# One core's attention and expert layers: the engines' orders run one group further ahead, with ScalarE's logarithm in front of the casts of a later group

## The chip, the cores and the metric

The kernel runs on one core of a Trainium2 chip. A core has TensorE (PE), VectorE (DVE), ScalarE (ACT), GpSimd (POOL) and SyncE (SP, which here only issues DMAs). Each engine works through its own list of instructions in order, and the lists meet in semaphores. The metric is the device time of one execution in microseconds (us), the median of several runs.

## The reference

Input is 8 sequences of 512 rows of 256 numbers. The first half is a causal attention layer with a layer norm, which the change doesn't touch. The second half, over the same 4096 rows, is an expert layer:

```python
logits = gelu(xf @ router_w1 + router_b1) @ router_w2 + router_b2   # two of 8 experts per row
for _ in range(2):                                                  # ITERS
    ctx = concat(integrated, v)
    shared_ctrl = gelu(ctx @ shared_w1 + b) @ shared_w2 + b
    x_sh, v_sh = inl(shared_ctrl, integrated, v, mu)
    ctrl = experts(ctx per chosen expert)                           # same shape, an expert's own weights
    x_r, v_r = inl(ctrl, ...), weighted sum over the two experts
    halt = sigmoid(gelu(integrated @ halt_w1 + b) @ halt_w2 + b)
    integrated, v += halt * (mix of shared and routed - old)
refined = gelu(integrated @ refine_w1 + b) @ refine_w2 + b
out = layernorm(x + xf + integration_weight * refined)

def inl(ctrl, xs, vs, mu):                                          # a, b, g: thirds of ctrl
    v_next = sigmoid(a) * vs - softplus(b) * (xs - mu)
    return xs + 0.1 * sigmoid(g) * v_next, v_next
```

## The kernel before

The function `experts` works in steps of 512 rows: a *group* is 512 rows in their own order (8 groups), a *quad* is 4 tiles of 128 rows sorted by expert, each tile with one expert's weights (18 quads). Its stages, one after the other, are: the router and the first shared pass; the first routed pass (18 quads, work numbers n from W_B); the second shared pass (8 groups, from W_S2); the second routed pass (18 quads, from W_D); and the refinement with the last norm (8 groups). The change touches the last four.

A step n of a pass goes through the engines like this.

- TensorE turns the rows (`turn`, L1941: transposes in fp32, 2 chunks in the first iteration, 4 in the second) into a ring of four PSUM banks (`ring`). The order of all fills of that ring is written out in the list FILLS (L1097).
- ScalarE casts each chunk to fp16 (`casts`, L1393). VectorE subtracts the cast from the chunk, which gives the low parts (`lows`, L1558), and with that frees the bank.
- TensorE makes the hidden layer from high and low parts (`routed_hidden`, L2047, 28 matmuls of 128 columns in the first routed pass and 52 in the second; `token_hidden`, L2093, 18 matmuls of 512 columns). For a quad it first reads the experts' numbers into registers (`quad_experts`, L2043). It begins only when all low parts are there (`ready`).
- ScalarE applies gelu twice (`gelu_hidden`, L1407: once in fp32, once in fp16), and VectorE makes the low half of the fp16 pair (`hidden`, L1567: a copy, L1570, and a subtraction, L1571).
- TensorE makes the control values (`control`, L1970) in two PSUM slots: two tiles to a slot in the first iteration, one in the second. A slot is free again when it has been read.
- ScalarE reads them (`tanhs`, L1431: tanh and, in the second iteration, relu for each of 4 tiles), loads the table of the logarithm, takes one logarithm over the step's 4 x 256 columns, and loads the gelu table again (`logs`, L1460). In front of the logarithm VectorE takes the absolute value in place (`absolute`, L1720).
- GpSimd subtracts and multiplies (`products`, L1294: two tensor_tensor instructions, L1300 and L1302). VectorE finishes the step (`velocity`, L1739, three instructions; `first_velocity` in the first iteration), and the result is stored, or added to the state (`add_shared2`, L1828).

In the second shared pass VectorE also adds up the routed results of the first iteration (`combine1`, L1804: 16 instructions a group, from rows that GpSimd gathers with indirect DMAs, `gather1`), and the halting gate is made: TensorE's `cl` fill (L2105), VectorE's `halts` (L1816), ScalarE's tanh (L1488), VectorE's `weigh` (L1824). The second routed pass gathers its rows with `gather_state` (L1327).

Before the change, the loop of each pass has in step n, on ScalarE: casts of step n+1, tanhs n, logs n, gelu n+1. On TensorE: turn n+1, control n, hidden n+1. On VectorE: lows n+1, absolute n, (combine1 n+2), velocity n-1, hidden n+1. The hidden pair h_hl, h_h1 has one buffer. In the refinement, a group's transposes, hidden layer and output follow each other on TensorE.

Of the kernel before, what the change touches and what calls it, by code (L numbers as in the profile page):

```python
# [868 lines left out]
def experts(nc, w, normed_dram, out):  # L869
# [7 lines left out]
    with ExitStack() as ctx:  # L877
# [63 lines left out]
        h_hl = sb("h_hl", [P, TOK], F16)  # L941
        h_h1 = sb("h_h1", [P, TOK], F16)
# [158 lines left out]
        for q in range(QUADS):  # L1101
            FILLS += [f"bx{q}_{c}" for c in range(KC)] + [f"bh{q}"]
        for g in range(GROUPS):
            FILLS += [f"cx{g}_{c}" for c in range(2 * KC)] + [f"cr{g}", f"cs{g}", f"cl{g}"]
        for q in range(QUADS):
            FILLS += [f"dx{q}_{c}" for c in range(2 * KC)] + [f"dh{q}"]
        for g in range(GROUPS):
            FILLS += [f"ex{g}_{c}" for c in range(KC)] + [f"eh{g}_{c}" for c in range(RC)]
# [118 lines left out]
        def _(pool):  # L1227
# [91 lines left out]
            for t in range(2 * NT):  # L1319
                gather1(t)  # L1320
            for g in range(GROUPS):
                for t in range((g + 2) * NT, min((g + 3) * NT, TILES)):
                    gather1(t)
                products(W_S2 + g, xs[:, g * NT:(g + 1) * NT, 0:D])


            def gather_state(q):  # L1327
                if q == 3:
                    pool.wait_ge(ew_done, W_D)
# [6 lines left out]

            for g in range(GROUPS):
                pool.wait_ge(xv_stored[g], 32)
            pool.wait_ge(comb_done, TILES)
            AHEAD = D_RING - 2  # L1340
            for q in range(AHEAD):
                gather_state(q)
            for q in range(QUADS):
                products(W_D + q, xg_it2(q)[:, :, 0:D])
                if q + AHEAD < QUADS:
                    gather_state(q + AHEAD)

# [29 lines left out]
        def _(act):  # L1377
# [96 lines left out]
            casts("b", 0, KC)  # L1474
            gelu_hidden(W_B, "bh0", h_hl[:], False)
            for q in range(QUADS):
                if q + 1 < QUADS:
                    casts("b", q + 1, KC)
                tanhs(W_B + q)
                logs(W_B + q)  # L1480
                if q + 1 < QUADS:
                    gelu_hidden(W_B + q + 1, f"bh{q + 1}", h_hl[:], False)

            def token_hidden(g):
                gelu_router(f"cr{g}", f"cl{g - 1}" if g else f"rl{GROUPS - 1}")
                gelu_hidden(W_S2 + g, f"cs{g}", h_hl[:], True)
# [3 lines left out]

            casts("c", 0, 2 * KC)
            token_hidden(0)
            for g in range(GROUPS):
                if g + 1 < GROUPS:
                    casts("c", g + 1, 2 * KC)
                tanhs(W_S2 + g)
                logs(W_S2 + g)
                if g + 1 < GROUPS:
                    token_hidden(g + 1)

            casts("d", 0, 2 * KC)
            gelu_hidden(W_D, "dh0", h_hl[:], False)
            for q in range(QUADS):
                if q + 1 < QUADS:
                    casts("d", q + 1, 2 * KC)
                tanhs(W_D + q)
                logs(W_D + q)
                if q + 1 < QUADS:
                    gelu_hidden(W_D + q + 1, f"dh{q + 1}", h_hl[:], False)
# [6 lines left out]
            act.wait_ge(ew_done, EWS)  # L1516
            for g in range(GROUPS):
                casts("e", g, KC)
                if g:
                    act.wait_ge(ctrl_filled[(uses(EWS) + g - 1) % 2], (uses(EWS) + g - 1) // 2 + 1)  # L1520
                    rstd(g - 1)
                for c in range(RC):
                    src, free = filled(f"eh{g}_{c}")
                    s.activation(gr32[:, c, :], src, ACT.Gelu, bias=cols[:, 2 + c:3 + c])
                    s.activation(gp[:, 0, c, :], src, ACT.Gelu, bias=cols[:, 2 + c:3 + c]).then_inc(free, 1)
            rstd(GROUPS - 1)

        @block.vector
        def _(dve):
# [259 lines left out]
            lows("b", 0, KC)  # L1789
            keep_ids(0)  # L1790
            hidden(W_B, "bh0", h_hl, h_h1)
            for q in range(QUADS):
                if q + 1 < QUADS:
                    lows("b", q + 1, KC)
                    keep_ids(q + 1)
# [4 lines left out]
                if q + 1 < QUADS:  # L1800
                    hidden(W_B + q + 1, f"bh{q + 1}", h_hl, h_h1)
# [35 lines left out]

            combine1(0)
            lows("c", 0, 2 * KC)
            combine1(1)  # L1840
            hidden(W_S2, "cs0", h_hl, h_h1)
            halts(0)
            for g in range(GROUPS):
                if g + 1 < GROUPS:
                    lows("c", g + 1, 2 * KC)
                absolute(W_S2 + g)
                weigh(g)
                if g + 2 < GROUPS:
                    combine1(g + 2)
                if g:  # L1850
                    velocity(W_S2 + g - 1, vs[:, (g - 1) * NT:g * NT, :])
                    add_shared2(g - 1)
                if g + 1 < GROUPS:
                    hidden(W_S2 + g + 1, f"cs{g + 1}", h_hl, h_h1)
# [344 lines left out]
```

## Time and profile before

| | us |
|---|---|
| median of 3 runs | 1744.98 (1744.79 to 1745.25) |
| the profiled execution's own time | 1741.15 |
| its span, first to last instruction | 1739.2 |
| first routed pass, first to last logarithm's end (842.10 to 1058.85) | 216.75 |
| second shared pass and the change-over, first logarithm's end to that of the second routed pass (1106.32 to 1306.71) | 200.39 |
| second routed pass, first to last logarithm's end (1306.71 to 1552.55) | 245.84 |
| rest to the end: last products, gathers, refinement | 186.65 |

The times of the stages are cut where ScalarE ends a logarithm, since each step has exactly one; 17 periods lie between the first and the last of 18. The last row of the table ends with the span.

### The profile page before, as it was taken

What the parts mean: (1) busy time and instruction counts of PE and PEld (TensorE: products, weight loads), DVE (VectorE), ACT (ScalarE), POOL (GpSimd) and SP (SyncE); (2) the same over time, 40 slices, a digit from 0 to 9 for tenths busy, and PEclk for the clock granted to TensorE, in tenths of its full rate; (3) what the DMA queues carried; (4) which work ended last, traced back from release to release, by engine and by line L of the source; (5) the groups of instructions that cost most, each with busy time, mean ns of one, the idle gap of its engine ahead of it and who ended that gap; (6) DMA issues with size and microseconds to landing.
All of it is one profiled execution on the core that took longest, in us unless ns stands there. A gap on an engine that the chain in (4) does not pass through costs nothing.

```text
span 1739.2 us, 21709 instructions
## 1 busy us (share of the span) xinstructions
PE 1085.2 (62%) x6930; PEld 648.3 (37%) x6930; DVE 1057.5 (61%) x1951; ACT 845.1 (49%) x1303; POOL 720.3 (41%) x692
## 2 busy tenths in 40 slices
PE   4778887978989456521556551654546666644775
PEld 2334453544544233200423231332225555532443
DVE  1655656666665337566465553888756777764665
ACT  1134534444545334354556652643547777751544
POOL 6012322223223360176233435645266666437451
PEclk9678988998989867665677775876768988876888
DMA  4946357176270395023243424544143333214341
GB/s 88 147 69 104 67 87 118 39 97 106 65 87 14 82 250 180 15 98 115 76 137 110 137 94 146 193 145 134 37 121 97 110 110 110 62 52 139 98 120 59
DMA packets 151755, 178.84 MB, mean 103 GB/s; under 512 B 33207, under 2 KB 127826, under 8 KB 151517
## 3 DMA queue, kind: packets, MB, share of 16 engines
q1 hardware_dynamic: 134624, 124.85, 31.6%
q0 software_dynamic: 17024, 52.58, 10.0%
q8 instruction: 66, 1.08, 0.3%
q14 instruction: 41, 0.34, 0.1%
HBM read 100.25 MB, written 76.87 MB: 102 GB/s over the span
## 4 chain that ended last, share of the span: by engine, by line
DVE 20%; PE 15%; ACT 13%; issue 10%; POOL 5%; DMA 2%; SPq 0%; ACTq 0%; DVEq 0%; POOLq 0%
PE exp_ps L1966 7%; DVE h_hl L1571 4%; ACT ct L1455 3%; DVE xs L1809 2%; DVE vs L1810 2%; PE exp_ps L2055 2%; ACT ct L1445 2%; PE exp_ps L2057 2%; ACT g L1413 1%; PE exp_ps L2056 1%; DVE h_h L1570 1%; ACT L1466 1%; PE exp_ps L2016 1%; DVE ct L1725 1%; ACT h_hl L1414 1%
## 5 line engine op out<-in xcount | busy, mean ns | idle before, releaser
L561 DVE TENSOR_REDUCE neg_max<-att_ps 128x1 f32<-128x512 f32 (+3 forms) x448 | 217.0, 533 | 75.5 <-PE att_ps L730 74.1
L499 ACT ACTIVATE probs<-att_ps 128x512 f32<-128x512 f32 x320 | 175.8, 609 | 172.1 <-PE att_ps L739 171.2
L1300 POOL TENSOR_TENSOR rb<-rb,ct 128x1024 f32<-128x1024 f32 x44 | 108.7, 2471 | 329.4 <-ACT ct L1465 329.4
L729 PE MATMUL att_ps<-k_stack,q_stack 96*128 96x512 bf16 (+3 forms) x512 | 163.3, 360 | 70.5 <-DVE neg_max L561 31.9
L1966 PE MATMUL exp_ps<-w_top,h_hl 128*128 (+2 forms) x280 | 102.1, 428 | 135.6 <-DVE h_hl L1571 117.7
L1399 ACT CAST e_xT<-exp_ps 128x512 f16<-128x512 f32 x172 | 92.5, 607 | 130.3 <-PE exp_ps L1944 130.1
L2055 PE MATMUL exp_ps<-e_xT,w 128*128 128x128 f16 x432 | 112.4, 266 | 57.0 <-issue 56.3
L406 POOL TENSOR_TENSOR wait_carrier<-wait_carrier 128x1 f32<-128x1 f32 x64 | 12.5, 195 | 297.4 <-ACT probs L499 297.4
L739 PE MATMUL att_ps<-q_stack,k_stack 98*128 98x512 bf16 (+3 forms) x512 | 125.4, 319 | 9.4 <-DMA q_stack<-max_parts 7.3
L730 PE MATMUL att_ps<-mask_q,identb 128*128 128x128 bf16 x512 | 126.5, 253 | 0.0
L1564 DVE TENSOR_TENSOR e_xT<-exp_ps,e_xT 128x512 f16<-128x512 f32 x172 | 109.8, 684 | 19.6 <-ACT e_xT L1399 18.2
L1291 POOL DMA_INDIRECT xs_dram<-xs,pos x64 | 68.1, 1064 | 108.7 <-DVE pos L1717 89.5
L2057 PE MATMUL exp_ps<-e_xT,w 128*128 128x128 f16 x432 | 111.8, 265 | 0.0
L2056 PE MATMUL exp_ps<-e_xT,w 128*128 128x128 f16 x432 | 111.1, 263 | 0.0
L729 PEld LDWEIGHTS att_ps<-k_stack,q_stack 96*128 96x128 bf16 x512 | 54.7, 110 | 144.3 <-DVE neg_max L561 93.4
L1445 ACT ACTIVATE ct<-exp_ps 128x1024 f32<-128x1024 f32 x52 | 53.2, 1024 | 110.4 <-PE exp_ps L1966 84.1
L1966 PE MATMUL exp_ps<-w_low,h_h 128*128 (+2 forms) x280 | 100.5, 422 | 0.0
L1966 PEld LDWEIGHTS exp_ps<-w_top,h_hl 128*128 128x128 f16 x280 | 30.0, 112 | 185.1 <-issue 164.0
L1944 PE MATMUL exp_ps<-e_ident,xs 128*128 128x128 f32 x192 | 32.4, 325 | 101.3 <-DVE vs L1810 68.1
L1455 ACT ACTIVATE ct<-exp_ps 128x768 f32<-128x768 f32 x104 | 84.6, 814 | 21.4 <-PE exp_ps L1966 20.4
L1725 DVE TENSOR_SCALAR ct<-ct 128x1024 uint32<-128x1024 uint32 x52 | 35.9, 690 | 95.9 <-ACT ct L1455 75.7
L411 POOL TENSOR_SCALAR_AFFINE_SELECT probs<-probs 128x640 f32<-128x640 f32 (+2 forms) x192 | 87.0, 486 | 0.0
(269 smaller groups left out, 3033.2 us busy)
## 6 DMA issues: line engine op xcount, KB each, us to landing
rs_dram<-rb SPq DMA_DIRECT2D x18, 1024.0 KB, 4.9
parts_dram<-parts SPq DMA_DIRECT2D x48, 256.0 KB, 2.6
q_stack<-parts_dram SPq DMA_DIRECT2D x96, 128.0 KB, 6.3
k_stack<-parts_dram SPq DMA_DIRECT2D x96, 128.0 KB, 9.9
xs_dram<-zeros SPq DMA_DIRECT2D x18, 520.0 KB, 9.8
xg<-xs_dram SPq DMA_DIRECT2D x18, 520.0 KB, 6.0
rs_dram<-rb SPq DMA_DIRECT2D x18, 512.0 KB, 2.9
x_in<-in_L_attn_encodings SPq DMA_DIRECT2D x8, 512.0 KB, 10.6
```

The source lines that it names most:

```text
L499: nc.scalar.activation(probs[:, pair % 4, u, :], src, ACT.Exp).then_inc(free, 1)
L561: return v.tensor_reduce(out, scores, AX.X, ALU.max, negate=True)
L729: t_.matmul(out, stationary, moving, start=True, stop=False)
L730: return t_.matmul(out[:, at:at + P], identb[:], mask, start=False, stop=True)
L739: return t_.matmul(out, k_stack[p][:, h, i * P:(i + 1) * P], q_stack[p][:, h, i * P:TOK], start=True, stop=True)
L1300: g_.tensor_tensor(m, m, b, ALU.subtract).then_inc(pool_step, 1)
L1455: last = s.activation(ct[:, par, i, :], raw, ACT.Tanh, scale=0.5)
L1564: v.tensor_tensor(xT[:, 1, c, :], ps[:, n % RINGS, :], xT[:, 0, c, :], ALU.subtract).then_inc(ring_freed[n % RINGS], 1)
L1966: last = t_.matmul(dst[:, a - parts[0][0]:z - parts[0][0]], stationary, moving[:, ds(w_at + a, z - a)], start=(j == 0), stop=(j == 1))
L2055: t_.matmul(o, hi, xT[:, 0, c, tok], start=(c == 0), stop=False)
L2056: t_.matmul(o, hi, xT[:, 1, c, tok], start=False, stop=False)
L2057: t_.matmul(o, lo, xT[:, 0, c, tok], start=False, stop=False)
```

## The change

Every engine's list in the four passes is written anew, so that the hidden layer of step n+1 comes in front of the control values of step n, and the transposes, casts and low parts belong to step n+2. h_hl and h_h1 get two buffers. The loops of the second shared and the second routed pass become one loop. On ScalarE the order in a step is gelu n+1, tanhs n, logs n, casts n+2. On VectorE `velocity` and `add_shared2` of step n-1 stand in front of `absolute` of step n. GpSimd gathers three quads' rows already in the second shared pass. In the refinement, the transposes of group g+1 come in front of the output of group g and the hidden layer g+1 behind it; VectorE takes the spread of a group as soon as it has its sum.

Buffers and the order of the ring's fills:

```diff
-        h_hl = sb("h_hl", [P, TOK], F16)
+        h_hl = sb("h_hl", [P, 2, TOK], F16)
...
+        for first, end in ((W_B, W_S2), (W_S2, EWS)):
+            FILLS += turn_fills(first) + hidden_fills(first) + turn_fills(first + 1)
+            for n in range(first, end):
+                FILLS += hidden_fills(n + 1) if n + 1 < end else []
+                FILLS += turn_fills(n + 2) if n + 2 < end else []
```

GpSimd:

```diff
+            for t in range(3 * NT):
+                gather1(t)
             for g in range(GROUPS):
...
+                for t in range((g + 3) * NT, min((g + 4) * NT, TILES)):
+                    gather1(t)
+                products(W_S2 + g, xs[:, g * NT:(g + 1) * NT, 0:D])
+                if GROUPS - 4 <= g < GROUPS - 1:
+                    gather_state(g - (GROUPS - 4))
+            gather_state(3)
```

ScalarE, the passes (of the three old loops the last is shown) and the refinement:

```diff
-            for q in range(QUADS):
-                if q + 1 < QUADS:
-                    casts("d", q + 1, 2 * KC)
-                tanhs(W_D + q)
-                logs(W_D + q)
-                if q + 1 < QUADS:
-                    gelu_hidden(W_D + q + 1, f"dh{q + 1}", h_hl[:], False)
...
+            for first, end in ((W_B, W_S2), (W_S2, EWS)):
+                turned(first)
+                hidden(first)
+                turned(first + 1)
+                for n in range(first, end):
+                    if n + 1 < end:
+                        hidden(n + 1)
+                    tanhs(n)
+                    logs(n)
+                    if W_S2 <= n < W_D:
+                        halt_gate(n - W_S2)
+                    if n + 2 < end:
+                        turned(n + 2)
...
+            casts("e", 0, KC)
             for g in range(GROUPS):
...
                 for c in range(RC):
                     src, free = filled(f"eh{g}_{c}")
                     s.activation(gr32[:, c, :], src, ACT.Gelu, bias=cols[:, 2 + c:3 + c])
                     s.activation(gp[:, 0, c, :], src, ACT.Gelu, bias=cols[:, 2 + c:3 + c]).then_inc(free, 1)
+                if g + 1 < GROUPS:
+                    casts("e", g + 1, KC)
+                if g:
+                    rstd(g - 1)
```

VectorE, the second shared and second routed pass, and the refinement:

```diff
+            def hidden2(n):
+                name = f"cs{n - W_S2}" if n < W_D else f"dh{n - W_D}"
+                hidden(n, name, h_hl[:, n % 2], h_h1[:, n % 2])
+                if n < W_D:
+                    halts(n - W_S2)
+
+            def update2(n):
+                if n < W_D:
+                    g = n - W_S2
+                    velocity(n, vs[:, g * NT:(g + 1) * NT, :])
+                    weigh(g)
+                    add_shared2(g)
+                else:
+                    velocity(n, xg_it2(n - W_D)[:, :, D:])
...
+            for n in range(W_S2, EWS):
+                if n + 1 < EWS:
+                    hidden2(n + 1)
+                if n > W_S2:
+                    update2(n - 1)
+                absolute(n)
+                if n + 2 < EWS:
+                    turned2(n + 2)
+                if n + 3 < W_D:
+                    combine1(n + 3 - W_S2)
...
             for g in range(GROUPS):
-                if g:
-                    lows("e", g, KC)
-                    steps = spread_of(g - 1)
                 refine_low(g)
+                if g + 1 < GROUPS:
+                    lows("e", g + 1, KC)
                 if g:
                     finish(g - 1, steps)
                 if g + 2 < GROUPS:
                     combine2(g + 2)
                 take(g)
-            finish(GROUPS - 1, spread_of(GROUPS - 1))
+                steps = spread_of(g)
+            finish(GROUPS - 1, steps)
```

TensorE:

```diff
+            for first, end in ((W_B, W_S2), (W_S2, EWS)):
+                turn_stage(first)
+                at = stage_hidden(first)
+                if first == W_S2:
+                    halt_logits(0)
+                turn_stage(first + 1)
+                for n in range(first, end):
+                    here = at
+                    if n + 1 < end:
+                        at = stage_hidden(n + 1)
+                    control(n, h_hl[:, n % 2], h_h1[:, n % 2], here)
+                    if W_S2 <= n + 1 < W_D and n + 1 < end:
+                        halt_logits(n + 1 - W_S2)
+                    if n + 2 < end:
+                        turn_stage(n + 2)
...
+            for g in range(GROUPS):
+                if g + 1 < GROUPS:
+                    turn_refined(g + 1)
+                refine_out(g)
+                if g + 1 < GROUPS:
+                    refine_hidden(g + 1)
```

`turned`, `turned2`, `turn_stage` are the casts, low parts and transposes of the pass to which n belongs; `hidden` and `stage_hidden` likewise. The first routed pass has the same loop on VectorE, with `relus`, `absolute` and `first_velocity` of n-1 in the middle.

## Rows read from the trace of the kernel before

**Rows 1.** Windows: stretch, length; busy us of PE, PEld, DVE, ACT, POOL; granted clock; DMA.

```profile
842.10:1058.85 216.75, 119.99 (x722) 69.06 (x720) 126.25 (x150) 132.00 (x151) 80.95 (x34) 0.74 0.34 110
...
1106.32:1306.71 200.39, 99.06 (x487) 61.40 (x485) 149.88 (x233) 94.52 (x150) 100.77 (x76) 0.71 0.35 110
1306.71:1552.55 245.84, 166.61 (x1402) 129.17 (x1400) 171.93 (x165) 183.06 (x285) 146.29 (x86) 0.89 0.31 91
```

**Rows 2.** Timeline, second routed pass, one period: start, us, engine, line, instruction [idle before].

```profile
1390.37 1.28 ACT L1463 ACT_TABLE_LOAD   x1
...
1390.72 1.22 DVE L1744 SCALAR_TENSOR_TENSOR ct<-ct,vs 128x1024 f32<-128x1024 f32 x1
...
1391.66 1.15 ACT L1465 ACTIVATE ct<-ct,half 128x1024 f32<-128x1024 f32 x1
...
1391.72 0.28 PE L2055 MATMUL exp_ps<-e_xT,w 128*128 128x128 f16 x1 [2.49 <-issue]
...
1392.89 2.51 POOL L1300 TENSOR_TENSOR rb<-rb,ct 128x1024 f32<-128x1024 f32 x1 [3.74 <-ACT ct L1465]
...
1394.68 0.31 PE L2057 MATMUL exp_ps<-e_xT,w 128*128 128x128 f16 x1
...
1395.48 3.24 POOL L1302 TENSOR_TENSOR rb<-rb,vs 128x1024 f32<-128x1024 f32 x1
...
1396.60 0.60 ACT L1413 ACTIVATE g<-exp_ps 128x512 f32<-128x512 f32 x1 [2.49 <-PE exp_ps L2058]
...
1397.57 2.06 ACT L1399 CAST e_xT<-exp_ps 128x512 f16<-128x512 f32 x4
...
1397.72 1.15 DVE L1570 COPY h_h<-h_hl 64x512 f16<-64x512 f16 x1 [1.23 <-ACT h_hl L1414]
...
1398.88 0.70 DVE L1571 TENSOR_TENSOR h_hl<-g,h_hl 64x512 f16<-64x512 f32 x1
...
1399.72 0.50 PE L1966 MATMUL exp_ps<-w_top,h_hl 128*128 x2 [1.31 <-DVE h_hl L1571]
...
1400.66 0.81 ACT L1455 ACTIVATE ct<-exp_ps 128x768 f32<-128x768 f32 x1 [1.03 <-PE exp_ps L1966]
```

**Rows 3.** Timeline, first routed pass, from one control to its logarithm.

```profile
949.72 0.61 PE L1966 MATMUL exp_ps<-w_top,h_hl 128*128 x1 [5.30 <-DVE h_hl L1571]
...
953.35 1.02 ACT L1445 ACTIVATE ct<-exp_ps 128x1024 f32<-128x1024 f32 x1 [0.60 <-PE exp_ps L1966]
...
955.73 1.15 ACT L1465 ACTIVATE ct<-ct,half 128x1024 f32<-128x1024 f32 x1
```

**Rows 4.** Timeline, second shared pass, part of one period.

```profile
1153.13 1.05 PE L2105 MATMUL exp_ps<-w2rh,rh 128*128 128x1 f32 x8 [1.78 <-ACT rh L1405]
...
1164.04 1.67 DVE L1834 SCALAR_TENSOR_TENSOR xs<-rb,nwx,xs 128x256 f32<-128x256 f32 x4
...
1166.97 0.21 ACT L1488 ACTIVATE gates_t<-gates 128x4 f32<-128x4 f32 x1 [12.73 <-DVE halt L1822]
...
1167.08 2.03 ACT L1399 CAST e_xT<-exp_ps 128x512 f16<-128x512 f32 x4
...
1167.68 2.48 DVE L1564 TENSOR_TENSOR e_xT<-exp_ps,e_xT 128x512 f16<-128x512 f32 x4 [0.74 <-ACT e_xT L1399]
```

**Rows 5.** The low parts' line (source view): count, min/median/max in ns.

```profile
L1564 DVE TENSOR_TENSOR e_xT<-exp_ps,e_xT x172: 678/681/693, 632.1 to 1714.8; 128x512 f16<-128x512 f32 x172
```

**Rows 6.** The chain that ended last, refinement: start, us, engine, line.

```profile
1636.01 5.11 DMA rb<-normed_dram
1641.20 2.54 POOL rb L1359
...
1653.11 2.69 DMA vs<-rs_dram,pos
...
1673.76 4.74 DMA rb<-normed_dram
```

**Rows 7.** The waits view: who waited for whom, us in total, times, longest.

```profile
DVE ct L1885 <- ACT ct L1525: 31.6, 28, 3.1
```

More of the change, by code:

```diff
@@ L1318, in _ @@
                 pool.wait_ge(rs_stored[i], 16 * stores_before(W_S2, i))
[L1319 to L1324, printed above, removed]
             def gather_state(q):
+                if q == 0:
+                    for g in range(GROUPS):
+                        pool.wait_ge(xv_stored[g], 32)
+                    pool.wait_ge(comb_done, TILES)
                 if q == 3:
@@ L1472, in _, with turned, hidden, halt_gate @@
                 logs(W_S1 + g)
-            casts("b", 0, KC)
-            gelu_hidden(W_B, "bh0", h_hl[:], False)
-            for q in range(QUADS):
-                if q + 1 < QUADS:
-                    casts("b", q + 1, KC)
-                tanhs(W_B + q)
-                logs(W_B + q)
-                if q + 1 < QUADS:
[L1482 to L1486, printed above, removed]
+            def turned(n):
+                if n < W_S2:
+                    casts("b", n - W_B, KC)
+                elif n < W_D:
+                    casts("c", n - W_S2, 2 * KC)
+                else:
+                    casts("d", n - W_D, 2 * KC)
+            def hidden(n):
+                if W_S2 <= n < W_D:
+                    g = n - W_S2
+                    gelu_router(f"cr{g}", f"cl{g - 1}" if g else f"rl{GROUPS - 1}")
+                    gelu_hidden(n, f"cs{g}", h_hl[:, n % 2], True)
+                else:
+                    gelu_hidden(n, f"bh{n - W_B}" if n < W_S2 else f"dh{n - W_D}", h_hl[:, n % 2], False)
+            def halt_gate(g):
                 act.wait_ge(gates_ready, g + 2)
@@ L1489, in token_hidden @@
                              scale=0.5).then_inc(gates_done, 1)
[L1491 to L1504, printed above, removed]
-                    casts("d", q + 1, 2 * KC)
-                tanhs(W_D + q)
-                logs(W_D + q)
-                if q + 1 < QUADS:
-                    gelu_hidden(W_D + q + 1, f"dh{q + 1}", h_hl[:], False)
+            for first, end in ((W_B, W_S2), (W_S2, EWS)):
[7 more added lines that the diff above has]
+                    logs(n)
+                    if W_S2 <= n < W_D:
+                        halt_gate(n - W_S2)
+                    if n + 2 < end:
+                        turned(n + 2)
             def rstd(g):
@@ L1799, in _ @@
                     first_velocity(W_B + q - 1)
[L1800 to L1801 removed]
+                if q + 2 < QUADS:
+                    turned1(q + 2)
             first_velocity(W_B + QUADS - 1)
@@ L1838, in _ @@
             combine1(0)
-            lows("c", 0, 2 * KC)
+            turned2(W_S2)
             combine1(1)
[L1841 to L1854, printed above, removed]
-                    halts(g + 1)
@@ L1856, in _ @@
-            velocity(W_S2 + GROUPS - 1, vs[:, (GROUPS - 1) * NT:, :])
-            add_shared2(GROUPS - 1)
-            lows("d", 0, 2 * KC)
-            hidden(W_D, "dh0", h_hl, h_h1)
-            for q in range(QUADS):
-                if q + 1 < QUADS:
-                    lows("d", q + 1, 2 * KC)
-                absolute(W_D + q)
-                if q:
-                    velocity(W_D + q - 1, xg_it2(q - 1)[:, :, D:])
-                if q + 1 < QUADS:
-                    hidden(W_D + q + 1, f"dh{q + 1}", h_hl, h_h1)
@@ L2107, in token_hidden @@
                 last.then_inc(done, 1)
-            turn_state(0)
-            token_hidden(0)
-            for g in range(GROUPS):
-                if g + 1 < GROUPS:
-                    turn_state(g + 1)
-                control(W_S2 + g, h_hl, h_h1, SHARED_AT)
-                if g + 1 < GROUPS:
-                    token_hidden(g + 1)
             def turn_sorted2(q):
@@ L2161, in _ @@
                 last.then_inc(done, 1)
+            turn_refined(0)
+            refine_hidden(0)
+            for g in range(GROUPS):
+                if g + 1 < GROUPS:
[3 more added lines that the diff above has]
+                    refine_hidden(g + 1)
 def build(nc, args, out):
```

109 lines of the change are left out of this document (58 added, 51 removed).

## The prediction

> **What bounds the kernel now.** I read the page first (no engine is busy for two thirds of the span, so the order of the work sets the time), then the chain that ended last, which shows the same few links in every step of a pass, then the windows cut at logarithms, which give each pass a period, and last the timeline of one period per pass. The times below are those of the profiled execution, 1741.15 us, 3.83 below the median of the runs; I add the difference of the two kernels to the median.
>
> The reader should look for the loop: what in step n must end before the same thing in step n+1 can begin.
>
> Second routed pass: 245.84 / 17 = 14.46 us a step [rows 1], of which ScalarE works 10.8 (183.06 / 17). Its logarithm ends at 1392.81, GpSimd's two products run back to back to 1398.72, and VectorE's copy L1570, which should be shorter than the 0.70 of the subtraction behind it, lasts 1.15 until just after that; then come the subtraction, TensorE's control at 1399.72, the first tanh at 1400.66, four tiles and the next table load 14.46 after 1390.37, the logarithm [rows 2]. So the loop is logarithm, products, hidden half, control, tanhs. The hidden matmuls run beside it: they begin at 1391.72 behind 2.49 us of register reads and end with gelu at 1396.60, 4.88 later; their 28th step falls at 1394.68, so they go at 0.106 us each, TensorE's half rate (1.2 of 2.4 GHz), until then [rows 2]. This second path is only about 0.9 us shorter than the first.
>
> First routed pass: 216.75 / 17 = 12.75 us a step [rows 1]. Control begins after 5.30 us of silence on TensorE, all of it at half rate; the second tanh waits until 3.63 after its start, and the logarithm begins 2.38 after that [rows 3]. Control, tanh, logarithm, gelu, hidden half, control is the loop.
>
> Second shared pass: ScalarE waits 12.73 us in a step for the halting gate, which stands on VectorE behind 16 combining instructions and the update [rows 4]; VectorE is busy for 149.88 of 200.39 us [rows 1].
>
> Refinement: every second group goes through the load of x, the residual sum on GpSimd, eight gathers, and only then VectorE, 37.75 us for two groups (1636.01 to 1673.76) [rows 6].
>
> **The change part by part.**
>
> The gelu of step n+1 no longer lies between logarithm n and control n+1 as the last link: the control values of n find their hidden half made a step earlier. That link (gelu, hidden half, the products' lock on it) goes from all three loops. But what is late next stands on ScalarE itself. Its order is gelu n+1, tanhs n, logarithm n, casts n+2, and then at once gelu n+2. Between these casts and that gelu lie the low parts on VectorE and the whole hidden layer on TensorE, and ScalarE has nothing to do meanwhile: everything behind this gelu in its list (tanhs, logarithm) waits too, and for these GpSimd and VectorE. Before, the logarithm and the tanhs covered the hidden layer. The register reads do go under cover (they stand in front of the wait for the low parts, beside table load and casts).
>
> *Second routed pass, from the end of a logarithm.* Table load 1.30; first low part 0.60 after the first cast (1167.08 to 1167.68) and four of them 2.48 [rows 4], ends at 4.38; to TensorE 0.14 (subtraction's end at 1399.58, control at 1399.72); hidden layer until gelu 4.88, at 9.40; two gelus 0.97 (1396.60 to 1397.57), at 10.4 [rows 2]. Control n+1 starts when the hidden layer ends and its first tile takes 0.94, so tanh follows gelu directly. Tanhs to table load 4.17, load 1.29, at 15.9 [rows 2]. VectorE meanwhile: hidden half 1.0 (the subtraction's 0.70 and 0.3 for a copy that meets no product), three velocity instructions of 1.25, absolute value 0.7, all after gelu: 16.0, just behind. Logarithm 1.15: 17.2 us against 14.46. Sixteen such periods and a last one of 10.5 (no casts, no hidden layer; but products, velocity, absolute, logarithm in a row) are 285.7 against 245.84: **+40 us**. Bounds: the hidden layer at half rate to its end, 52 x 0.106 = 5.5, gives +50; at the full level throughout, half of that, gives +6. I take 4.88, since the silence ahead of it will be some 6 us and the row already starts at half rate after 2.49.
>
> *First routed pass.* Load 1.30, two low parts 1.84, 0.14, hidden layer 28 x 0.106 = 2.97, then control. Half rate throughout gives 3.63 to the second tanh, full rate half of the matmuls' part, 1.9; I take 2.75 (the clock rises somewhere in it). Then 2.38 and 1.15 [rows 2, 3]. Sum 12.6 (11.7 to 13.4) against 12.75: a wash, -2. The extra hidden layer and gelu ahead of the first tanhs cost 3.5, the last period saves 3 (no casts, but it waits for the store of two steps before). **-2 us, -14 to +10.**
>
> *Second shared pass.* Load 1.30, gate 0.11, low parts 3.08, 0.14 [rows 4]; 18 matmuls of 512 columns, 7.6 at half rate, 3.8 at full, taken as 5.9; gelus 1.2: 11.8. The third control tile waits for the first tanh and relu, the fourth is issued at about 14.7; the halting logits are behind it, 1.05, and VectorE waits for them ahead of everything else: 16.2. The update that now stands in front of the absolute value is 3.75 + 1.67 + 0.4 [rows 2, 4]: 22.0; absolute and logarithm: 23.8. The 16 combining instructions (at the 0.42 of the four adds in [rows 4], 6.7) run during the hidden layer and are hidden by it; without that cover they would add up to 4. Six periods of 23.8 and two of 19.4 at the change-over (no halting logits to wait for) are 181.6 against 200.39: -19; the second hidden layer ahead of the first tanhs adds 7. The saving is mostly the change-over: gathers for the second routed pass are done before it begins. **-12 us, -20 to -3.**
>
> *Refinement.* The chain over two groups has 19.8 us of load, residual, gathers (1636.01 to 1655.80) and 18 of VectorE's work [rows 6]. In the second, VectorE waits for gelus, 31.6 us in all over seven groups, 4.5 a group [rows 7]. In the new order the hidden layer and gelus of a group are done while the gathers run, so one wait in each pair goes, less 0.9 for the casts that now stand behind the gelus: three pairs x 3.6, 3 in the first group, and 3 in the last two groups, where no gather is waited for. **-17 us**, between 0 and -31.6.
>
> The gathers moved into the second shared pass (12, some 1.5 us each by the eight between 1643.74 and 1655.80 [rows 6]) find GpSimd idle there. A second buffer for the hidden pair costs nothing.
>
> Sum: +40 - 2 - 12 - 17 = **+9**; the few tenths by which semaphores add to such sums, over 40 periods of new chains, are an estimate of +2. 1745 + 11 = **1756 us**.
>
> The load at 1390.37 is followed by the logarithm at 1391.66, 1.29 later [rows 2]: no pause stands behind a load of 1.28. The Trainium skill, "ScalarE: Activation LUTs", section "What ACT_TABLE_LOAD costs", puts a switch of table set at that load and about 1.38 us of drain, 2.66 in all. By it both loads, now in one row with everything else on the loop, would make its period 2.8 longer, and the second routed pass would cost +84 instead of +40. I go by the row.
>
> **The rivals.**
>
> *The clock comes up sooner (other side).* If TensorE ran the hidden layers at its full level from the start, the second routed pass would lose 2.1 a step, the first 0.9, the second shared pass 2 in six steps: 16 x 3.0 + 12 = 60 less, 1696. Against it: half rate after 2.49 and after 5.30 us of silence [rows 2, 3], and granted clocks of 0.89, 0.74 and 0.71 [rows 1] with silences that the change makes longer. It decides from a sixth of those 60 on: there the kernel is no slower. A quarter or more of it: chance 0.08. About a sixth, or as much from the refinement beyond its 17: no change, 0.12.
>
> *Low parts blocked.* They now fall beside GpSimd's products, which stretch VectorE's copy in [rows 2]. If they waited for both products (2.51 and 3.24), each step of the routed passes would be 2.4 longer: 16 + 16 steps, +77, 1833. Against it: 172 of them take 678 to 693 ns [rows 5], with no stretched one. 0.03.
>
> *A pause after each table load.* If a load were followed by a pause of its own length, 1.28, wherever it is on the loop, each of 40 steps would take 2.6 more, 102, about 1858. The next instruction 1.29 after a load speaks against it [rows 2]. 0.01. It is what the rule of the Trainium skill cited above would have; with its figure it would be 110.
>
> *My forecast*, 0.76: gelu's wait for the hidden layer sets the period. Its own range is 1743 to 1771: the square root of the squares of the terms' half ranges (routed passes 10 and 9, shared 7, refinement 5 around its value).
>
> **How the numbers follow.** 1756 is the forecast's. A measurement of this kernel can tell about 0.2%, 3.5 us, from no change. Slower: 0.76 + 0.03 + 0.01 = 0.80; same 0.12; faster 0.08. Range 1740 to 1773: the forecast's own, taken down into the rival with the clock, leaving about 0.2 out.
>
> **What would show it.** In the second routed pass, periods of about 17 us between logarithms, ScalarE idle some 5.5 to 6 us ahead of gelu for the hidden matmuls (L2058), VectorE's copy L1570 shorter than the subtraction, GpSimd's products unstretched at about 2.4 each. In the first, the same wait of about 3.5 us and a period near 12.7. In the second shared pass, absolute as the releaser of the logarithm. In the refinement, the waits for L1525 cut to less than half. I am wrong if ScalarE doesn't wait ahead of gelu, if the hidden layers run at full rate, or if the refinement's gain reaches the second routed pass's loss.

## The result, and the profile after

The changed kernel takes 1752.72 us (median of 20 runs, 1746.04 to 1761.97) where the kernel before, run beside it, takes 1741.64 (20 runs, 1736.09 to 1749.49). The ratio is 1.0065, with a 95% interval of 1.0048 to 1.0083: slower by 11 us (8 to 15). The profiled execution took 1751.68 us with a span of 1749.6, the granted clock 0.789 against 0.798.

A small difference, and large ones beneath it. The windows view of the changed kernel, cut at ends of logarithms as in [rows 1] (first routed, second shared, second routed pass):

```profile
833.85:1049.84 215.99, 107.51 (x704) 76.35 (x704) 117.04 (x148) 131.27 (x149) 79.59 (x34) 0.72 0.34 110
1105.26:1289.25 183.99, 92.58 (x516) 54.56 (x516) 112.79 (x220) 92.41 (x150) 83.58 (x63) 0.77 0.30 94
1289.25:1579.03 289.78, 159.39 (x1344) 128.78 (x1344) 128.11 (x164) 182.06 (x283) 134.24 (x92) 0.78 0.28 84
```

| stretch (profiled executions) | before | after | difference | forecast |
|---|---|---|---|---|
| second routed pass | 245.84 | 289.78 | +43.9 | +40 |
| first routed pass, with the 35 us ahead of its first logarithm | 252.2 | 252.2 | 0.0 | -2 |
| change-over to the second shared pass (its first logarithm) | 47.47 | 55.42 | +8.0 | +7 |
| second shared pass, to the next pass's first logarithm | 200.39 | 183.99 | -16.4 | -19 |
| refinement, to the end | 186.6 | 170.6 | -16.1 | -17 |
| sum of what the change touches | | | +19.4 | +9, +2 for semaphores |
| everything earlier, which it doesn't touch | 806.7 | 797.7 | -9.0 | 0 |

The last line is dealt with below (e4, e8): executions of the same code differ by as much there.

The second routed pass, one period. This is the timeline of the changed kernel that answers to [rows 2]:

```profile
1399.29 0.29 PE L2076 MATMUL exp_ps<-e_xT,w 128*128 128x128 f16 x1 [6.69 <-DVE e_xT L1575]
...
1402.03 0.28 PE L2076 MATMUL exp_ps<-e_xT,w 128*128 128x128 f16 x1
...
1404.16 0.60 ACT L1425 ACTIVATE g<-exp_ps 128x512 f32<-128x512 f32 x1 [6.28 <-PE exp_ps L2079]
...
1405.28 0.28 DVE L1581 COPY h_h<-h_hl 64x512 f16<-64x512 f16 x1 [6.35 <-ACT h_hl L1426]
...
1409.31 1.28 ACT L1475 ACT_TABLE_LOAD   x1
...
1409.96 0.69 DVE L1736 TENSOR_SCALAR ct<-ct 128x1024 uint32<-128x1024 uint32 x1
...
1410.68 1.15 ACT L1477 ACTIVATE ct<-ct,half 128x1024 f32<-128x1024 f32 x1
...
1411.85 1.28 ACT L1478 ACT_TABLE_LOAD   x1
...
1411.91 2.34 POOL L1310 TENSOR_TENSOR rb<-rb,ct 128x1024 f32<-128x1024 f32 x1 [7.67 <-ACT ct L1477]
...
1413.14 2.05 ACT L1411 CAST e_xT<-exp_ps 128x512 f16<-128x512 f32 x4
...
1413.76 2.48 DVE L1575 TENSOR_TENSOR e_xT<-exp_ps,e_xT 128x512 f16<-128x512 f32 x4 [3.11 <-ACT e_xT L1411]
...
1416.60 0.29 PE L2076 MATMUL exp_ps<-e_xT,w 128*128 128x128 f16 x1 [6.69 <-DVE e_xT L1575]
```

Read it as a loop. ScalarE's logarithm, second load, casts; VectorE's low parts; TensorE's hidden layer after 6.69 us of silence, at 0.106 us a matmul until 1402.03; gelu, for which ScalarE has been idle for 6.28; tanhs; the first load. One turn is 1399.29 to 1416.60, 17.31. What went out of the loop can be seen too: the copy takes 0.28 (1.15 in [rows 2]) and GpSimd's products 2.34 each (2.51 and 3.24): they don't meet any more. No time was gained by it, since the links that went were replaced by longer ones.

The first routed pass and the second shared pass, from the timeline (answering to [rows 3] and [rows 4]):

```profile
953.24 0.29 PE L2076 MATMUL exp_ps<-e_xT,w 128*128 128x128 f16 x1 [6.39 <-DVE e_xT L1575]
...
956.52 0.60 ACT L1425 ACTIVATE g<-exp_ps 128x512 f32<-128x512 f32 x1 [4.32 <-PE exp_ps L2079]
...
961.77 1.15 ACT L1477 ACTIVATE ct<-ct,half 128x1024 f32<-128x1024 f32 x1 [0.18 <-DVE ct L1736]
...
964.23 1.07 ACT L1411 CAST e_xT<-exp_ps 128x512 f16<-128x512 f32 x2
...
1193.62 0.16 DVE L1837 TENSOR_TENSOR gates<-exp_ps,b2rh 128x4 f32<-128x4 f32 x1 [2.63 <-PE exp_ps L2115]
...
1199.47 0.69 DVE L1736 TENSOR_SCALAR ct<-ct 128x1024 uint32<-128x1024 uint32 x1
1200.20 1.15 ACT L1477 ACTIVATE ct<-ct,half 128x1024 f32<-128x1024 f32 x1 [4.97 <-DVE ct L1736]
...
1203.37 2.48 DVE L1575 TENSOR_TENSOR e_xT<-exp_ps,e_xT 128x512 f16<-128x512 f32 x4 [3.21 <-ACT e_xT L1411]
```

The same loop in the first pass (gelu waits 4.32). In the shared pass the logarithm waits 4.97 for absolute, which stands behind the halting logits and the update. The second shared pass, up to the next pass's first logarithm, is 16.4 us shorter; 15.7 of these lie in its last two periods (17.75 and 38.01 before, 19.90 and 20.21 after), the change-over; how much of that is the early gathers and how much the merged loop was not tested. The waits view puts the whole wait for the hidden layers of both routed passes under one line, about 5.4 us in each of 36 steps. The wait of [rows 7] is gone: the source view names no releaser any more for VectorE's line that waited there (L1906 now).

```profile
ACT g L1425 <- PE exp_ps L2079: 193.1, 36, 7.2
```

The refinement in the chain that ended last (answering to [rows 6]): two groups take 1640.15 to 1675.61, 35.46, where they took 37.75; the last two groups, 1714.60 to 1740.32, take 25.7, where they took 33.0 (1696.94 to 1729.91, the second fence, from the timeline of the kernel before).

```profile
1640.15 4.56 DMA rb<-normed_dram
...
1675.61 4.57 DMA rb<-normed_dram
...
1714.60 1.23 DVE rb L1914
...
1740.32 1.24 DVE rb L1914
```

```profile
1696.94 1.22 DVE L1893 TENSOR_TENSOR rb<-exp_ps,rb 128x1024 f32<-128x1024 f32 x1
...
1729.91 1.23 DVE L1893 TENSOR_TENSOR rb<-exp_ps,rb 128x1024 f32<-128x1024 f32 x1 [2.44 <-PE exp_ps L2160]
```

### The profile page after: what moved, and what is told of

Same layout as the page of the kernel before. It is cut to its first block, busy times and chain, and to the rows that moved or that the text cites. A ratio compares the mean times of both kernels' runs of the same rounds, so it can differ in the third digit from the quotient of the medians.

```text
span 1749.6 us, 21701 instructions
## 1 busy us (share of the span) xinstructions
PE 1056.1 (60%) x6930; PEld 652.7 (37%) x6930; DVE 976.9 (56%) x1951; ACT 845.8 (48%) x1303; POOL 697.7 (40%) x692
## 3 DMA queue, kind: packets, MB, share of 16 engines
q8 instruction: 66, 1.08, 0.3%
## 4 chain that ended last, share of the span: by engine, by line
DVE 21%; PE 16%; ACT 13%; issue 8%; POOL 4%; DMA 2%; SPq 1%; DVEq 0%; ACTq 0%; POOLq 0%
DVE e_xT L1575 5%; ACT L1478 3%; PE exp_ps L2076 3%; PE exp_ps L2077 2%; PE exp_ps L2078 2%; PE exp_ps L1987 2%; ACT ct L1457 2%; ACT ct L1477 2%; DVE ct L1736 2%; DVE rb L1757 2%; DVE ct L1755 2%; DVE rb L1759 2%; ACT e_xT L1411 2%; ACT g L1425 1%; ACT ct L1467 1%
## 5 line engine op out<-in xcount | busy, mean ns | idle before, releaser
L2076 PE MATMUL exp_ps<-e_xT,w 128*128 128x128 f16 x432 | 124.8, 294 | 233.6 <-DVE e_xT L1575 233.6
L1310 POOL TENSOR_TENSOR rb<-rb,ct 128x1024 f32<-128x1024 f32 x44 | 102.9, 2339 | 365.3 <-ACT ct L1477 365.3
L2076 PEld LDWEIGHTS exp_ps<-e_xT,w 128*128 x432 | 57.1, 132 | 244.0 <-issue 242.3
L2077 PE MATMUL exp_ps<-e_xT,w 128*128 128x128 f16 x432 | 125.1, 295 | 0.0
L2078 PE MATMUL exp_ps<-e_xT,w 128*128 128x128 f16 x432 | 124.3, 294 | 0.0
L1581 DVE COPY h_h<-h_hl 64x512 f16<-64x512 f16 x44 | 12.6, 286 | 187.0 <-ACT h_hl L1426 187.0
L1425 ACT ACTIVATE g<-exp_ps 128x512 f32<-128x512 f32 x36 | 21.5, 597 | 193.1 <-PE exp_ps L2079 193.1
L1987 PE MATMUL exp_ps<-w_top,h_hl 128*128 (+2 forms) x280 | 90.3, 383 | 31.5 <-ACT rb L1470 29.3
L1987 PE MATMUL exp_ps<-w_low,h_h 128*128 (+2 forms) x280 | 86.9, 371 | 0.0
L1477 ACT ACTIVATE ct<-ct,half 128x1024 f32<-128x1024 f32 x52 | 59.7, 1148 | 51.6 <-DVE ct L1736 50.1
```

The costliest lines, as they stand in the source:

```text
L1310: g_.tensor_tensor(m, m, b, ALU.subtract).then_inc(pool_step, 1)
L1987: last = t_.matmul(dst[:, a - parts[0][0]:z - parts[0][0]], stationary, moving[:, ds(w_at + a, z - a)], start=(j == 0), stop=(j == 1))
L2076: t_.matmul(o, hi, xT[:, 0, c, tok], start=(c == 0), stop=False)
L2077: t_.matmul(o, hi, xT[:, 1, c, tok], start=False, stop=False)
L2078: t_.matmul(o, lo, xT[:, 0, c, tok], start=False, stop=False)
```

## The experiments

The theory: with ScalarE's order gelu n+1, tanhs n, logarithm n, casts n+2, gelu n+2, the low parts and the hidden layer lie bare between the casts and the next gelu. The rivals: the bare time is only TensorE's low clock; something else sets the period and the wait is slack; the small sum hides a fault in the account.

**e1: casts of n+2 in front of the logarithm, second routed pass alone.**

```diff
                     tanhs(n)
+                    early = n + 2 < end and n + 2 >= W_D
+                    if early:
+                        turned(n + 2)
                     logs(n)
...
-                    if n + 2 < end:
+                    if n + 2 < end and not early:
                         turned(n + 2)
```

> The changed kernel, but in the second routed pass ScalarE's casts of step n+2 stand in front of the logarithm of n. Theory (gelu waits for a hidden layer that nothing covers): the casts begin at tanhs' end, 5.1 us after gelu; the low parts then stand behind VectorE's absolute value, 6.4 to 9.0; hidden layer 9.1 to 14.0 or 14.7 beside table load, logarithm, table load; period 14.0 to 14.7 against 17.3 to 17.5, some 48 us less in that pass, the other stages as in the changed kernel; about 1705. Rival (VectorE's update in front of the absolute value sets the period: gelu, hidden half, velocity, absolute, logarithm): that order stays, period stays at 17.3, about 1753. Rival (the clock: the colder TensorE is the cost): the silence ahead of the hidden layer falls from 6.7 to 3.4 us, the layer still starts at half rate, period falls by under 1 us, about 1740.

Measured: 1696.33 us, ratio to the kernel before 0.9725 (0.9692 to 0.9759). Its windows and one period:

```profile
1287.49:1528.26 240.77, 160.50 (x1344) 128.93 (x1344) 126.31 (x163) 178.44 (x279) 139.13 (x92) 0.85 0.34 101
```

```profile
1399.97 2.06 ACT L1411 CAST e_xT<-exp_ps 128x512 f16<-128x512 f32 x4
...
1401.49 2.48 DVE L1578 TENSOR_TENSOR e_xT<-exp_ps,e_xT 128x512 f16<-128x512 f32 x4
1402.05 1.28 ACT L1475 ACT_TABLE_LOAD   x1
1403.34 1.15 ACT L1477 ACTIVATE ct<-ct,half 128x1024 f32<-128x1024 f32 x1
...
1404.32 0.29 PE L2079 MATMUL exp_ps<-e_xT,w 128*128 128x128 f16 x1 [3.61 <-DVE e_xT L1578]
```

The low parts now run beside the first load, and the hidden layer begins before the second load, where in the changed kernel it begins 4.75 us after it (1411.85 to 1416.60). The pass loses 49.0 us (289.78 to 240.77), all that the change had added to it and 5 more. The total falls 9 us below what was expected: another 7 go at the change-over, where the last two periods ahead of the second routed pass's first logarithm are 16.5 and 16.8 instead of 19.9 and 20.2. TensorE's clock is not what changed: the layer still starts at 0.106 us a matmul after 3.61 us of silence, and takes 4.73 to 5.76 us to gelu, as in the changed kernel (4.73 to 5.77). Order alone removed the loss.

**e2: TensorE kept busier ahead of its silence.** The transposes of the second routed pass are each done three times over.

```diff
-            turn(f"dx{q}_{c}", lambda t: xg_it2(q)[:, t, c * P:(c + 1) * P])
+            turn(f"dx{q}_{c}", lambda t: xg_it2(q)[:, t, c * P:(c + 1) * P], 3)
```

> The changed kernel with each transpose of the second routed pass made three times (the same result written again), so that TensorE's silence ahead of the hidden layer falls from 6.7 to under 3 us with nothing else moved. Theory (the exposed hidden layer, of which half rate is only a part): the layer to gelu falls from 4.9 to 5.9 us at most to 2.9 where TensorE comes at full rate, period 17.4 to 15.3, 30 to 35 us less; still above 14.46. Rival (the clock is the whole loss): period back at 14.5 or below, 48 us less. If the layer still starts at half rate: no change, and the price of the clock stays unmeasured.

Measured: 1747.63 us, ratio 1.0042 (1.0020 to 1.0065), an interval that overlaps the changed kernel's. The windows view and the timeline:

```profile
1289.93:1580.07 290.14, 211.95 (x1824) 179.80 (x1824) 128.12 (x164) 182.12 (x283) 134.64 (x92) 0.88 0.28 84
```

```profile
1391.29 5.40 PE L1965 MATMUL exp_ps<-e_ident,xg 128*128 128x128 f32 x48
...
1399.89 0.28 PE L2076 MATMUL exp_ps<-e_xT,w 128*128 128x128 f16 x1 [3.20 <-DVE e_xT L1575]
...
1402.72 0.28 PE L2076 MATMUL exp_ps<-e_xT,w 128*128 128x128 f16 x1
...
1404.86 0.60 ACT L1425 ACTIVATE g<-exp_ps 128x512 f32<-128x512 f32 x1 [6.38 <-PE exp_ps L2079]
```

The pass is unchanged (290.14 against 289.78), though its mean granted clock rose from 0.78 to 0.88: the silence is cut from 6.69 to 3.20, but the layer behind it still starts at 0.106 us a matmul and keeps that until 1402.72. What was gained in clock fell where nobody waits. This run says nothing on what a layer wholly at the full rate would give.

**e3: the refinement's new order alone, put into the kernel before** (its hunk of the diff, and nothing else).

> The kernel before with the new order of the refinement alone (ScalarE, VectorE, TensorE), the four passes as before. Theory (one wait for gelus in each pair of groups, and those of the last two groups, go): from the last logarithm of the second routed pass to the end 187 becomes about 171, 16 us less in all, about 1726 against a before of 1742. Rival (that stretch is shorter only because the passes in front of it end differently): no gain, 1742.

Measured: 1720.76 us, ratio 0.9866 (0.9833 to 0.9899), 18 to 29 us faster. The refinement takes 170.1 us from the last logarithm (1551.58) to the end (1721.7), as in the changed kernel.

**e4: the kernel before once more**, one execution, for the 9 us in the part that the change doesn't touch.

> The kernel before once more, profiled, to see how far the stages that the change does not touch move from execution to execution. The end of the last logarithm of the first shared pass stood at 806.7 us in the profile of before and at 797.7 in that of the changed kernel, 9.0 earlier, with the same instructions. If that is the spread of single executions: anywhere between 795 and 812 here. If the change shortens that part: 806 to 807 again.

Measured: 1743.6 us; the last logarithm of the first shared pass ends at 804.63. That part's end lies at 806.66, 804.63 and 806.09 (e3) in executions of the old code, and at 797.67, 798.32, 805.79, 807.27, 804.06, 803.85 and 806.75 in the changed kernel, e2, e1, e5, e6, e7 and e8, which share its code up to there. Seven executions of one code span 10 us by themselves; the three of the old code lie within 2 us of each other, and five of the seven lie within 1 us of them, so the 9.0 is no sign of the change, though a small part of it isn't excluded. The refinement spreads as well: 186.6, 192.0 and (e8) 187.3 in the old order, 165.1 to 170.6 in seven executions of the new, 188.6 against 168.5 on average.

**e5: casts in front of the logarithm in all three merged passes** (the condition of e1 without its last term).

> The changed kernel with the casts of n+2 in front of the logarithm of n in all three merged loops (e1 did so in the second routed pass alone: 1696 us). Theory (ScalarE's order, with low parts and hidden layer bare between logarithm and next gelu, sets each loop): in the first routed pass the low parts then follow VectorE's velocity instead of the casts behind the second table load, about 1.9 us earlier a step, 16 steps, -30; in the second shared pass the low parts come 3.3 earlier, but the combining instructions behind them then run beside GpSimd's products and stretch, so 2.4 a step, 6 steps, -14. About 1652 us. Rival one (the first routed pass is set by control and tanhs, and gelu's wait is only slack): 1682, with its period still 12.7. Rival two (the combining instructions, stretched, set the second shared pass): 1666, with its period still 23.8.

Measured: 1637.21 us, ratio 0.9388 (0.9329 to 0.9447): the fastest kernel of the study, and 15 below what was expected. Windows (first routed, second shared), then the timeline of each:

```profile
844.63:1016.16 171.53, 95.86 (x699) 72.52 (x697) 120.23 (x145) 127.98 (x147) 79.81 (x34) 0.83 0.43 139
1072.24:1227.02 154.78, 88.78 (x512) 53.28 (x510) 124.99 (x216) 93.09 (x150) 86.51 (x63) 0.81 0.37 112
```

```profile
960.77 0.60 ACT L1425 ACTIVATE g<-exp_ps 128x512 f32<-128x512 f32 x1 [2.46 <-PE exp_ps L2082]
...
966.09 1.15 ACT L1477 ACTIVATE ct<-ct,half 128x1024 f32<-128x1024 f32 x1
...
966.31 1.28 DVE L1578 TENSOR_TENSOR e_xT<-exp_ps,e_xT 128x512 f16<-128x512 f32 x2
...
1152.81 2.34 POOL L1310 TENSOR_TENSOR rb<-rb,ct 128x1024 f32<-128x1024 f32 x1 [4.30 <-ACT ct L1477]
1153.86 1.57 DVE L1830 SCALAR_TENSOR_TENSOR xs<-xg,nwx,xs 128x256 f32<-128x256 f32 x1
1155.36 2.56 DVE L1831 SCALAR_TENSOR_TENSOR vs<-xg,nwx,vs 128x256 f32<-128x256 f32 x1
```

In the first routed pass the low parts start 0.2 after the logarithm's start instead of 3.1, and the period falls to 10.2 (2.75 less, where 1.9 was expected); gelu's wait goes from 4.32 to 2.46. In the shared pass the period is 20.5 instead of 23.9. The stretched combining instructions are there (1.57 and 2.56 us, 0.48 without a product beside them), but only two of sixteen are stretched in the step shown.

**e6: absolute of n in front of the update of n-1, second shared pass alone.**

```diff
+                if n < W_D:
+                    absolute(n)
                 if n > W_S2:
                     update2(n - 1)
-                absolute(n)
+                if n >= W_D:
+                    absolute(n)
```

> The changed kernel, with VectorE's absolute value of n in front of the update of n-1 in the second shared pass alone. The changed kernel's logarithm waits there 5 us for absolute, which stands behind the update. If the update were the loop and nothing else met it, logarithm and casts would come 5 earlier and the low parts 3.1 earlier (the update must still end first): six steps, -19, about 1734 us. If the update's two-input instructions are stretched by GpSimd's products, which then start beside them (1.22 to 3.25 us each as velocity instructions were in the kernel before), the low parts come only 0.7 earlier: -4, about 1748. I expect the second. Rival (the wait for absolute is slack and the hidden layer sets the period): 1752, with unstretched updates.

Measured: 1755.59 us, ratio 1.0075 (1.0046 to 1.0104): no gain. Absolute is at the head, the logarithm follows the table load without a wait, and the period is still 24:

```profile
1176.17 0.16 DVE L1837 TENSOR_TENSOR gates<-exp_ps,b2rh 128x4 f32<-128x4 f32 x1 [2.63 <-PE exp_ps L2118]
1176.38 0.69 DVE L1736 TENSOR_SCALAR ct<-ct 128x1024 uint32<-128x1024 uint32 x1
...
1179.02 2.64 POOL L1310 TENSOR_TENSOR rb<-rb,ct 128x1024 f32<-128x1024 f32 x1 [7.09 <-ACT ct L1477]
...
1179.49 3.25 DVE L1759 SCALAR_TENSOR_TENSOR rb<-ct,rb 128x1024 f32<-128x1024 f32 x1
...
1181.74 3.20 POOL L1312 TENSOR_TENSOR rb<-rb,xs 128x1024 f32<-128x1024 f32 x1
...
1182.66 2.30 DVE L1660 TENSOR_SCALAR halt<-gates_t 128x4 f32<-128x4 f32 x1
...
1186.79 2.48 DVE L1575 TENSOR_TENSOR e_xT<-exp_ps,e_xT 128x512 f16<-128x512 f32 x4
```

The wait was 5 us long and its removal worth nothing, not even the 4 us that were expected: the products now run beside the update, which is stretched, so the rival with unstretched updates doesn't hold either. The last velocity instruction takes 3.25 instead of 1.22, and a multiplication over four columns, 0.16 before, takes 2.30. The low parts begin at 1186.79, 10.62 after the halting logits (1176.17); in the changed kernel they begin 9.75 after them (1193.62 to 1203.37, shown above).

**e7: a shorter hidden layer.** In the second routed pass 16 of its 52 matmuls are left out (low parts of the weights by high parts of the inputs).

```diff
-                        t_.matmul(o, lo, xT[:, 0, c, tok], start=False, stop=False)
+                        if chunks == KC:
+                            t_.matmul(o, lo, xT[:, 0, c, tok], start=False, stop=False)
```

> The changed kernel; in the second routed pass the hidden layer leaves out 16 of its 52 matmuls (the products of the weights' low parts with the inputs' high parts). Theory (gelu's wait for the hidden layer is on the loop of the period of 17.3 us): the layer begins at the half rate for some 26 matmuls (0.106 us each) and ends at the full rate, so 16 fewer save about 1.4 us a step (0.9 all at full rate, 1.7 all at half), and the period falls by as much: 17 steps, -23 (-15 to -29), about 1730 us. Rival (VectorE's velocity and absolute, or the table loads, set the period, and the hidden layer is beside them): no change, 1752, ScalarE's wait ahead of gelu just moves to the wait ahead of the logarithm.

Measured: 1735.64 us, ratio 0.9973 (0.9945 to 1.0002), 17 less than the changed kernel's median. The pass takes 276.32 us, 13.5 less, 0.8 a step: on the loop, but at the low end.

```profile
1393.31 0.29 PE L2076 MATMUL exp_ps<-e_xT,w 128*128 128x128 f16 x1 [6.67 <-DVE e_xT L1575]
...
1397.13 0.85 PE L1987 MATMUL exp_ps<-w_top,h_hl 128*128 x2
...
1397.38 0.60 ACT L1425 ACTIVATE g<-exp_ps 128x512 f32<-128x512 f32 x1 [5.47 <-PE exp_ps L2080]
```

In this step all 36 matmuls go at 0.106 (3.82 in all): the layer is over before the clock rises, and the half rate runs on into the control matmuls (0.85 for a pair that takes 0.50 in the changed kernel). The time saved is that of the matmuls which in the changed kernel run last and at the full rate.

**e8: the changed kernel with the refinement's order put back.**

> The changed kernel with the refinement's order put back to that of the kernel before, and nothing else. Theory (the change is a sum of a loss of 36 us in the merged passes, +44 in the second routed pass, -1 in the first, +8 and -16 around the second shared one, and of a gain of 17 to 22 in the refinement that e3 measured alone; the two don't touch each other): 1752 + 20 = 1772 us, 31 to 35 above the kernel before. Rival one (part of the 9 us that the changed kernel's profile was earlier at the end of the first shared pass belongs to the change): about 1764. Rival two (the refinement's new order gains less behind the slower second routed pass than alone): 1757 to 1765.

Measured: 1774.83 us, ratio 1.0184 (1.0133 to 1.0234), 31.8 above the kernel before, with the refinement at 187.3 us again. The profiled execution ends its first shared pass at 806.75, as the kernel before does at 806.66, and there the stretches after it add 33.4 us to those of the kernel before, the whole difference of the two spans (1772.7 and 1739.2). So loss and gain add up, within the 23 to 41 us that the interval of the ratio leaves.

## Why the prediction was right

1756 was forecast and 1752.72 measured; the mechanism is the one that was named. That the total came so close is in part luck. Against the kernel before, 11 us were forecast and 11.1 measured in the medians. But the stages that the change touches add 19.4 in the two profiled executions, and the earlier part takes 9.0 of that back by its spread. As averages over all profiled executions in which a stage is as in either kernel, the stages add some 14 (second routed pass +43.9, first +0.4, second shared with its change-over -10.4, refinement -20.1). And of the 11 that were forecast, 2 were put down to semaphores, a term that no row shows.

*Second routed pass, +40: measured +43.9.* The loop is the one written down: first low part 0.62 after the casts begin, hidden layer from 1399.29 to gelu at 1404.16, 4.87 (4.88 in the forecast, from [rows 2]), absolute's end at 1410.65 level with the table load's at 1410.59. The last period is 10.4 (10.5 forecast). The 4 us over come from the sixteen full periods: 17.46 on average ((289.78 - 10.4)/16), from 17.2 to 18.2, instead of 17.2. The trace shows where they lie. From its first matmul to gelu the layer takes 4.73 us in the shortest of the sixteen steps and 5.77 in the longest, in which all 52 matmuls go at 0.106; in every one of them the period is that time and 12.4 to 12.5 more (layer and period: 5.77 and 18.20, 5.43 and 17.87, 4.87 and 17.31, 4.73 and 17.17). So the period follows the layer one for one, and the layer follows the point at which the clock rises. On average the layer takes 5.02, 0.14 more than forecast; the hand-over from the last low part to TensorE takes 0.36 (1416.24 to 1416.60), where 0.14 had been taken from another pair of instructions; 0.1 of these 0.36 the forecast had made up for by rounding. e1 removes the whole loss by order, e7 shows again that the hidden layer is on the loop; the rivals of e1 and e7 by which gelu's wait is slack fall.

*First routed pass, -2: measured 0.* A wash, but out of terms that were off and cancel, which is luck. The period is 12.95 on average instead of 12.6, and gelu waits 4.32 where 3.5 was forecast: the layer takes 3.28 to gelu in the step shown, not 2.97, since the forecast counted its matmuls alone. The last period is 8.8 instead of some 9.8, and the additional hidden layer ahead of the first tanhs costs 0.7 instead of 3.5. In most steps the layer is over before the clock rises; it rises in the control behind it, which takes 1.89 us in the shortest step and 3.41 in the longest, with periods of 12.0 and 13.5.

*Second shared pass, -12: measured -8.4* (+8.0 and -16.4). Absolute is the releaser of the logarithm, with periods of 23.9 to 24.1 (23.8) and 19.9 to 20.2 at the change-over (19.4).

*Refinement, -17: measured -16.1* in the profiled executions, -20 as an average over ten. Counted in the two profiled ones at the addition of each group's output (L1893 before, L1914 after), the first group gives 0.4 from the last logarithm on (3 forecast), the second 4.6, the two pairs after it 2.3 and 1.6 (3.6 forecast for each pair), and the last two groups 7.3 (3). Right in sum, and misplaced. That the last groups gain most because no gather is in their way is not tested.

*Table loads.* The step at 1411.85 is followed by the casts at 1413.14, 1.29 later, now with both loads on the loop, and the period is 17.3 and not 2.8 longer. The Trainium skill, "ScalarE: Activation LUTs", section "What ACT_TABLE_LOAD costs", would have 2.66 for a switch; here the measurement decides against it.

*The clock.* That rival was not borne out: the layers start at the half rate after 6.4 to 6.7 us of silence, and still do after 3.61 (e1) and 3.20 (e2).

*Low parts beside products.* They take 2.48 for four with a product beside them (1413.76 against 1411.91 to 1416.67), so that rival falls too. Velocity instructions, combining instructions and the copy are stretched, and e6 shows the price. The Trainium skill, "SBUF — State Buffer", section "Who interferes with whom", has the pattern: VectorE with two inputs in SBUF contends with a GpSimd instruction that reads SBUF, and whichever comes second is blocked; with at most one (the low parts read one input from PSUM) it doesn't, outside the modes that use two ports. e6 agrees: the velocity instruction that begins at 1179.49 ends 1.08 after the product beside it (1182.74 and 1181.66), and the next product takes 3.20 instead of 2.34.

*Sums.* Three figures don't come out of the prediction's own terms; none of them moved the 1756. Blocked low parts: waiting for products of 2.51 and 3.24 from 1.9 us behind the logarithm on would cost 3.9 a step, not 2.4. The first routed pass: 16 periods of 11.7 give -16 as the lower bound, not -14. The forecast's own range: the half ranges 10, 9, 7 and 5 make 16, where 1743 to 1771 is 14 to either side, and they are narrower than the bounds stated stage by stage (+6 to +50 is 22 to either side).

What stays open is where the spread of 10 us in the first 800 us comes from, and what a hidden layer at the full rate throughout would give. For that there is only an estimate: from 1402.14 on the matmuls of the step shown go at 0.056 us each, 52 of them would take 2.9, and gelu some 0.2 more. Against 5.02 that is 1.9 a step, 30 of the 44 us if the period follows one for one so far down, so the low clock alone would not be the whole loss.

## What to carry to other kernels

To issue work a step ahead helps only as far as each in-order engine has something to do while it is under way: write down for every engine what stands between the last instruction that the early work needs and the first that needs its result. Here the same change with one group of instructions in front of the logarithm instead of behind it is 6% faster than the kernel it started from (e5; some 20 of its 101 us are the refinement's, by e3), and as made 0.7% slower. A wait of 5 us can be worth nothing if what comes earlier by it stretches the instructions it now runs beside (e6), and a small sum should be taken apart into its stages before it is called small.

## What was not expected of the hardware

A multiplication of 128 x 4 elements on VectorE took 2.30 us beside GpSimd's product, 0.16 without, and ended when the product did (1184.96 and 1184.94): what the meeting cost went by the other instruction's length, not by its own. And 16 of 52 matmuls left out saved only half of what the mean rate (4.87/52, 0.094 each, 1.5 in all) gives, since the clock rose later in the step's work or not at all within the layer.
